# A hybrid layer stack on one core: the order of the side work in the first phase's scan loop

## The reference

```
x = x + mamba_and_ffn(layernorm(x))
x = x + gates(layernorm(x));  x = x + attention(layernorm(x));  x = x + gates(layernorm(x))

mamba_and_ffn(x):
  h  = layernorm(x)*ln1_g + ln1_b
  xi, z = split(rmsnorm(h, rms_w) @ in_proj_w)
  xc = silu(causal_conv4(xi) + conv_b)
  dbc = xc @ x_proj_w
  delta = softplus(dbc[:64] @ dt_proj_w + dt_b);  B, C = rest of dbc (16 states each)
  s[t] = exp(delta*A)*s[t-1] + delta*xc*B[t];   y[t] = sum over states of s[t]*C[t]
  h  = h + ((y + D*xc) * silu(z)) @ out_proj_w
  x  = x + h;   x = x + relu((layernorm(x)*ln2_g+ln2_b) @ ffn_w1 + b1) @ ffn_w2 + b2
gates: c = sigmoid(f)*c + sigmoid(i)*tanh(g) over the items, f, i, g from x and c;
       out = tanh(x @ wo + c_final @ uo + bo)
```

## Time and profile before

| | us |
|---|---|
| median of 3 runs | 1742.65 (1741.66 to 1743.93) |
| the profiled execution | 1739.67 |
| its span (first to last instruction) | 1737.8 |
| VectorE busy | 1223.2 (70%) |
| TensorE matmul busy | 1401.7 (81%) |
| ScalarE busy | 873.0 (50%) |
| GpSimd busy | 653.4 (38%) |

### The profile page before, as it was taken

How to read it: one execution, slowest core, us unless ns; L and a number is a source line. 1 busy time by engine, 2 the same in 40 slices (tenths; PEclk the granted TensorE clock), 3 DMA queues, 4 the chain that set the end, 5 groups by cost and what they waited for, 6 DMA issues and landing times. The chain is left out here.

```text
span 1737.8 us, 17267 instructions
## 1 busy us (share of the span) xinstructions
PE 1401.7 (81%) x5520; PEld 663.3 (38%) x5520; DVE 1223.2 (70%) x1907; ACT 873.0 (50%) x1496; POOL 653.4 (38%) x335
## 2 busy tenths in 40 slices
PE   2324678979797979898973799999999999999994
PEld 1101243545454444545541233444343434343432
DVE  2398999898989898973124887676766767666425
ACT  3545565656574847352120365555555564645533
POOL 3466767666584847571124321211222121200000
PEclk9656888989998999999996699999999999999997
DMA  5415151423324141501026333333333332320034
GB/s 166 166 43 181 38 193 51 141 103 109 121 84 160 46 150 66 169 34 37 12 85 133 74 74 76 89 71 80 70 89 71 86 75 62 72 58 9 26 113 154
DMA packets 93785, 158.03 MB, mean 91 GB/s; under 512 B 8592, under 2 KB 74704, under 8 KB 90576
## 3 DMA queue, kind: packets, MB, share of 16 engines
q1 hardware_dynamic: 93696, 156.94, 30.8%
HBM read 110.91 MB, written 46.01 MB: 90 GB/s over the span
## 5 line engine op out<-in xcount | busy, mean ns | idle before, releaser
L1225 DVE TENSOR_REDUCE mx<-psum 128x1 f32<-128x512 f32 x512 | 345.6, 687 | 209.1 <-PE psum L1710 206.8
L1476 ACT ACTIVATE pw<-psum 128x512 f32<-128x512 f32 x512 | 300.1, 597 | 315.6 <-PE psum L1725 314.6
L862 POOL TENSOR_TENSOR hb<-ddb,bcb 128x1024 f32<-128x1024 f32 x128 | 303.8, 2389 | 130.1 <-DMA ddb<-dd 58.0
L518 DVE TENSOR_TENSOR_SCAN psum<-psum,hb 128x512 f32<-128x512 f32 x224 | 261.9, 1214 | 54.8 <-ACT psum L704 32.0
L1710 PE MATMUL psum<-kp,qp 96*128 96x512 bf16 x512 | 204.1, 400 | 46.6 <-DVE mx L1225 25.2
L704 ACT ACTIVATE psum<-ddb,A_neg 128x512 f32<-128x512 f32 x256 | 164.6, 679 | 97.3 <-DVE hb L521 55.9
L1725 PE MATMUL psum<-qp,kp 99*128 99x512 bf16 x512 | 197.7, 387 | 7.2 <-ACT pw L1476 6.0
L1618 POOL TENSOR_TENSOR rstd<-rstd,neg_half 128x4 f32<-128x4 f32 x16 | 16.3, 1018 | 413.3 <-DVE rstd L1210 413.3
L1736 PE MATMUL psum<-pw,v_sb 128*32 128x512 f32 x1024 | 137.2, 608 | 3.5 <-DVE ot L1249 2.1
L521 DVE TENSOR_TENSOR hb<-psum,bcb 128x1024 f32<-128x1024 f32 x112 | 137.2, 1225 | 3.9
L921 PE MATMUL psum<-back,w 128*128 128x512 f32 x256 | 117.1, 612 | 2.8 <-ACT middle L681 1.7
(11 more groups left out here) (184 smaller groups left out, 2152.0 us busy)
## 6 DMA issues: line engine op xcount, KB each, us to landing
ddb<-dd SPq DMA_DIRECT2D x64, 512.0 KB, 7.6
bcb<-bc SPq DMA_DIRECT2D x32, 512.0 KB, 6.1
parts<-parts_sb SPq DMA_DIRECT2D x96, 128.0 KB
dd<-dd_out SPq DMA_DIRECT2D x8, 1024.0 KB, 4.1
qp<-parts SPq DMA_DIRECT2D x32, 256.0 KB, 7.9
kp<-parts SPq DMA_DIRECT2D x16, 384.0 KB, 4.7
x_front<-x_dram SPq DMA_DIRECT2D x8, 512.0 KB, 3.9
xh<-x_front SPq DMA_DIRECT2D x8, 512.0 KB, 5.1
```

The lines of the kernel that those rows point to most:

```text
L518: e.tensor_tensor_scan(to[:, g, :], a[:, g, :], h[:, g, :], 0.0, ALU.mult, ALU.add).then_inc(scan_ok, 1)
L862: e.tensor_tensor(hb[n % NHB], ddb[k % NSLOT][:, 1:2, :].to_broadcast([P, 2, L]), bcb[q][:, 0, :, :], ALU.mult).then_inc(bx_ok, 1)
L1225: used.up(e.tensor_reduce(mx[u % 2][:, n:n + 1], bank(used.n % 2), AXIS.X, ALU.max))
L1476: e.activation(pw[n % NPW], bank(5 + n % 2), ACT.Exp, scale=HD ** -0.5).then_inc(exp_ok, 1)
```

## The change

Nothing is computed otherwise, and no instruction is added or removed. The places in the scan loop are new for these:

- VectorE: `back_sum` from after unit 2 to after unit 1, `back_moments` from after unit 3 to after unit 2 (GpSimd's power for it with it); the three softplus operations from after unit 10 to after unit 11 and `gated(i, 0)`. `gate_state` waits for its tanh half by half.
- ScalarE: `gate_xwo` one unit earlier and ahead of `mid_th`; `mid_th` one unit later; `back_apply` ahead of `gate_i`; relus 6 and 7 ahead of the softplus functions; the half of `front_apply` that writes `x_front` (now `front_norm`) after the decay of unit 11.
- GpSimd: the product `mid_du` one unit later; the addition into `x_front` (now `front_sum`) from the end of `front_scale` to after `front_rms` at unit 12.

```diff
@@ dve_first
+                ring_done(e, "gf", b, 1)
                 for f in range(NF):
-                    e.wait_ge(gth_ok, 4 * b + 4)
+                    e.wait_ge(gth_ok, 4 * b + 3 + f)
...
+                    if u == 1 and back:
+                        back_sum(i - 1)
                     if u == 2 and back:
-                        back_sum(i - 1)
+                        back_moments(i - 1)
...
-                    if u == 3 and back:
-                        back_moments(i - 1)
...
-                    if u == 10 and mid:
-                        mid_soft(i + 1)
                     if u == 11 and s:
                         gated(i, 0)
+                    if u == 11 and mid:
+                        mid_soft(i + 1)
@@ act_first
                 ins.then_inc(h_raw, 1)
+
+            def front_norm(b):
                 for t in range(NT):
...
-                    if u == 2 and mid:
+                    if u == 2 and gate:
+                        gate_xwo(i - 2)
+                    if u == 3 and mid:
                         mid_th(i + 1)
-                    if u == 3 and gate:
-                        gate_xwo(i - 2)
+                    if u == 3 and back:
+                        back_apply(i - 1)
                     if u == 4 and gate:
                         gate_i(i - 2)
-                    if u == 4 and back:
-                        back_apply(i - 1)
...
-                    if u == 9 and mid:
-                        mid_soft(i + 1)
                     if u == 9 and back:
                         back_relu(i - 1, 6)
                         back_relu(i - 1, 7)
+                    if u == 9 and mid:
+                        mid_soft(i + 1)
+                    if u == 10 and front:
+                        front_norm(i + 2)
@@ pool_first
                 e.tensor_tensor(tok(T0), tok(T0), over_tiles(row("ln1_b")), ALU.add).then_inc(h_ok, 1)
+
+            def front_sum(b):
                 e.wait_ge(h_ok, b + 1)
                 e.wait_ge(xn_ok, b + 1)
                 e.tensor_tensor(x_front, x_front, tok(T0), ALU.add).then_inc(xh_ok, 1)
...
+                    if u == 2 and back:
+                        norm_power(0, b_var, i, b_rstd)
                     if u in (1, 2) and mid:
                         e.wait_ge(conv_ok, 2 * (i + 1) + u)
-                    if u == 3 and back:
-                        norm_power(0, b_var, i, b_rstd)
...
-                    if u == 10 and mid:
-                        mid_du(i + 1)
                     if u == 9 and front:
                         front_scale(i + 2)
+                    if u == 11 and mid:
+                        mid_du(i + 1)
                     if u == 12 and front:
                         front_rms(i + 2)
+                        front_sum(i + 2)
```

## The result

The changed kernel takes 1754.13 us (median of four runs, 1752.66 to 1755.84) against 1742.16 of the kernel before beside it; the ratio is 1.0070, 95% interval 1.0052 to 1.0088. The change makes the kernel slower by some 12 us. The forecast was 1737.6: wrong in sign, and the time lies above the range. The profiled span is 1750.9 us, 13.1 more than the 1737.8 of before.

What follows compares the result with a forecast made beforehand. VectorE set the period before; after the change SyncE's queue would bound full periods. Gains and losses over all stretches summed to -5.1 us: 1742.65 - 5.1 = 1737.6 us, range 1725 to 1749.

Steps and rivals of the forecast that it cites:

- Unit 10 at 50.4: VectorE in a full period: unit 10 would start 50.4 us after unit 0's start, where it was 58.1.
- +0.5: VectorE beside the convolution: 0.5 us allowed per full period for GpSimd's moved `back_moments` power getting in its way.
- The waits of 1.42 us ahead of unit 6 and 4.68 ahead of unit 10: VectorE's waits for ScalarE in item 3: the first would go; of the second 4.0 would go, 0.7 stay.
- Line 499 and the statistics behind it: 1.4 us gone: VectorE ahead of unit 10: 1.4 us saved per full period, between 0 and 2, from fewer GpSimd products there.
- 84.9 less 3.8: VectorE's busy time per full period, less time behind GpSimd; with waits of 0.7 and 4.7 it would finish at 87.
- The half clock's 2.0 per period: TensorE idle at the period's start would run `w_out` at half clock, adding 2.0 us to VectorE's chain, 2.3 at most.
- du 16.7 behind unit 10, the addition 10.4 behind du, the landing 2.9: Full-period chain: `du` starts at 67.1 us, `xh_ok` comes at 77.5, then the `xh` store lands 2.9 later.
- The rival of a late landing: The `xh` store takes 5.1 us even alone, each of five transitions 2.2 longer: 1751 us, chance 0.15.
- The row of loads, 9.6: SyncE's queue after the `xh` landing: four loads taken as 9.6 us, from 9.35 to 9.8, before GpSimd's first product.
- Item 0, +8.3: Item 0: later `du` and `xh_ok` put the next unit 0 at 167.7 instead of 159.4, 8.3 us longer.
- Ahead of the first unit, +0.9: Before the first unit: the addition behind the power, ahead of the first in_proj and first `ddb`, costs 0.9 us.
- Item 7, -5.7: Item 7, paced by TensorE: `back_apply` ahead of `gate_i` saves 2.74 idle and 1.7 at half clock, `back_sum` 1.2.

Runs made afterwards that it cites:

- e1: Changed kernel, with SyncE's loads for units 0 and 1 of the next item ahead of the `xh` store and `x_front` load: 1718.70 us, ratio 0.9855.
- e11: Changed kernel, with only ScalarE's softplus functions moved behind the decay of unit 11: 1726.66 us, ratio 0.9907.
- e12: Changed kernel, with the four next-item loads between the `xh` store and the `x_front` load in SyncE's order: 1737.73 us, ratio 0.9970.
- e14: Kernel before, with only the `x_front` part and the next-item loads ahead of the `xh` store: 1729.27 us, ratio 0.9922.
- e7: Kernel before, with only the reordered back and gate parts; softplus, `du` and `x_front` stay: 1711.36 us, ratio 0.9812.
- e8: Changed kernel, with GpSimd's product for unit 8 placed behind the front item's power: 1745.00 us, ratio 1.0006.
- e4: Kernel before, with only VectorE's softplus and GpSimd's `du` one unit later, ScalarE's functions behind relus 6 and 7: 1761.18 us, ratio 1.0097.
- e3: Kernel before, with only the `x_front` part: line 626 operations at unit 10, addition behind `front_rms`: 1749.52 us, ratio 1.0039.
- e10: Kernel before, with the reordered back and gate parts and the next-item loads ahead of the `xh` store: 1710.34 us, ratio 0.9810.
- e6: Changed kernel, with next-item loads ahead of the `xh` store and ScalarE's softplus functions behind the decay of unit 11: 1690.76 us, ratio 0.9698.
- e9: Changed kernel, with next-item loads ahead, ScalarE's softplus functions behind unit 11's decay, GpSimd's unit 8 product behind the front power: 1688.48 us, ratio 0.9687.

## Why the prediction was wrong, by its own steps

- **The mechanism held.** Softplus behind unit 11, `du`, the late addition, the store, the loads, a wait of unit 0 for GpSimd and that for `ddb`: every link and its order is in the trace, and e1, e11, e12 and e14 each move the time the way it says.
- **Unit 10 at 50.4: the step that failed.** It starts at 53.9 on average of items 1 to 5. Up to unit 4 the row came out as forecast (+0.4 for +0.5). Behind it three terms of the sum were mis-sized.
  - The waits of 1.42 us ahead of unit 6 and 4.68 ahead of unit 10 were read in item 3, where both are the longest of the five full periods. On average they were 0.6 and 3.9 before, and of the second 1.0 stays. So the stretch from unit 4 to 6 gained 2.0 for 2.8, and that from unit 7 to 10 gained 2.9 for 4.0.
  - "Line 499 and the statistics behind it: 1.4 us gone, since fewer GpSimd products lie there" is wrong in sign: +0.5. Line 499 became shorter, 2.1 to 1.3 us on average, but line 464 met a product in every period in place of two of five, 1.0 to 2.3 us on average. I had looked at which GpSimd products leave the place, not at which arrive when VectorE itself comes earlier.
  - VectorE's busy time says the same: the prediction took 84.9 less 3.8, that is 81.1 us; it is 83.4.

  Unit 10 of the kernel before, in items 1 and 4:

```profile
216.75 2.35 DVE L518 TENSOR_TENSOR_SCAN psum<-psum,hb 128x512 f32<-128x512 f32 x2 [2.92 <-ACT psum L704]
...
496.39 2.35 DVE L518 TENSOR_TENSOR_SCAN psum<-psum,hb 128x512 f32<-128x512 f32 x2 [3.53 <-ACT psum L704]
```

- **The half clock's 2.0 per period** was there at TensorE (`w_out` 5.18 to 6.78 us at the start of items 1 to 5, after 3.66 to 8.48 us idle), and cost VectorE about 1.0 by the nearest comparison: from unit 0 to unit 4 it took 26.2 us, in e7 with `w_out` at 3.72 it took 25.2. In e1, also with `w_out` at 3.72, it took 26.6, with GpSimd beside the convolution, so what the half clock costs by itself is not shown. The +0.4 up to unit 4 includes it, where the forecast had +0.5 and another 2.0: this error went the other way, so that 1.5 of the 3.5 us is left.
- **du 16.7 behind unit 10, the addition 10.4 behind du, the landing 2.9:** measured 16.8, 10.3 and 2.9 each time. The rival of a late landing, priced at 1751, came near the time by a cause that is not there. The fit of the Trainium skill, "DMA: Bandwidth & Descriptors", Anatomy of one DMA, from which the prediction has its estimate of 3.2 us is given there for transfers that GpSimd issues; these are SyncE's, and the sum went by the trace's 2.9.
- **The row of loads, 9.6:** 10.0 to 10.2 in items 1 to 4, 11.1 in item 0. I took it from item 0 of before, and from the lower end. With it items 1 to 4 are 2.1 each over the 94.4, item 5 2.8 over its 91.2: the 11 us of the table.
- **Item 0, +8.3:** measured 10.6; 1.5 by the loads, 0.9 by a later `du`.
- **Ahead of the first unit, +0.9:** measured +3.9. TensorE did `w_xp` and `w_dt` here in 3.73 and 3.78 us, where before it did them in 1.96 and 1.98. That makes ScalarE's softplus functions 3.3 us later and is not put down to the change (last section). What the change itself does comes to about +0.6: the first in_proj 2.1 later, behind the addition; the second addition 3.1 later, behind `du`; the landing 2.2 shorter; the 2.0 of line 626 gone from the row; and 0.3 less in line 505 and the loads.
- **Item 7, -5.7:** measured -2.9. The gap in TensorE ahead of the first feed-forward product is 3.37 us, ended by ScalarE's `back_turned`, where 2.74 stood; I had let it go altogether. **Behind the last scan** it did go, 5.7 for 5.9:

```profile
769.69 15.70 PE L929 MATMUL psum<-back,w 128*128 128x512 f32 x32 [3.37 <-ACT back L723]
...
840.89 14.00 PE L929 MATMUL psum<-back,w 128*128 128x512 f32 x32 [1.24 <-ACT back L723]
```

- **Item 6, -2.9:** measured -2.4.
- **The range.** The prediction said itself that each us of period error counts five times, and yet gave everything slower than 1746 only 0.15. Its sum of -5.1 was the difference of gains and losses several times that size, all in one chain, and the load row stood at its lower end. Order alone is worth 33 us, softplus alone costs 17: a sum with such parts is not known to 10 us. And what made the sum so poor was visible in it: it ended in "the queue becomes the bound" with VectorE standing still, so that no gain on VectorE behind `du` could count any longer.
- **Still open:** why the row of loads took 12.1 to 12.3 us at item 1 in e8 and e11 and 10 to 11 elsewhere in these two.

## What to carry to other kernels

When a change makes the critical engine's row shorter and moves a producer later in the same edit, work out where the transfers behind that producer then stand, and move them in the queue with it: the four loads ahead of a store that needn't be waited for were worth 35 us here, and some 4 in the kernel before. Try the parts of such a change by themselves: one was worth 33 us, two cost 17 and 7, and all three lost 12. Price an operation that two engines share time on by what will stand beside it afterwards, not by what leaves. And read a wait in every period before using it for all: item 3's were the longest of five.

## What the runs showed of the hardware

- The store of `xh` landed after 5.06 to 5.69 us each time it left within half a us of the 1 MB store of `dd_out` (before, and in e4), and after 2.90 to 2.93 us each time it left alone, 3.5 us or more behind it (after, e3, e8, e11). In e1, where it left some 3 us behind the loads of `ddb`, it took 4.17 to 5.24 us at the ends of items 0 to 4.
- A VectorE operation of 0.15 us can take 2.33, ending when GpSimd's product does. GpSimd's product is lengthened too: in e8, beside VectorE's line 499 and statistics, it took 3.33 us in place of 2.35.
- TensorE's clock ahead of the first unit is not settled by what a kernel does there. The same four `w_xp` products took 1.96 us behind 3.37 us of idle time in before, 3.73 behind 3.07 in the changed kernel, 1.96 behind 3.56 in e10 and 3.65 behind 2.55 in e8. The programs of e6 and e9 are the same up to there, and these are their rows:

```profile
43.88 1.96 PE L929 MATMUL psum<-xc,w_xp 128*96 128x512 f32 x4 [3.40 <-DVE xc L495]
```

```profile
44.41 3.73 PE L931 MATMUL psum<-xc,w_xp 128*96 128x512 f32 x4 [3.17 <-DVE xc L495]
```

  The windows of these products in before and after show a granted clock of 1.00 (2.4 GHz) and 0.50 (1.2 GHz):

```profile
42.20:44.20 2.00, 1.96 (x4) 0.57 (x4) 1.19 (x2) 0.78 (x1) 0.00 (x0) 1.00 0.00 0
```

```profile
44.40:48.10 3.70, 3.68 (x4) 0.91 (x4) 2.92 (x9) 0.71 (x1) 0.00 (x0) 0.50 0.00 0
```

  Differences of up to 3.6 us ahead of the first unit are therefore not put down to an edit here. By the Trainium skill, "TensorE: Matmul & The Clock Gate", Part 1, the array falls to half clock when it has been idle; the rows agree that it does, and show that idle time alone doesn't say whether it does.
